# Channel attention on pairs of images, with the second image's gathers held for the next pair's first convolution

## What is computed

```python
xn = (x - mu) * rsqrt(var + EPS) * ln_g + ln_b          # mu, var over one whole image
def _proj(xn, wp, bp, wd, bd):
    y = einsum('bhcij,hoc->bhoij', xh, wp) + bp         # 8 heads of 12 channels
    return dwconv3x3(y, wd, bd)
Q, K, V = _proj(xn, ..q..), _proj(xn, ..k..), _proj(xn, ..v..)
logits = einsum('bhnc,bhnd->bhcd', K, Q) / alpha        # n: the 256 pixels
attn = softmax(logits, axis=-1)
out = einsum('bhnc,bhcd->bhnd', V, attn)
return einsum('bcij,oc->boij', out, w_f) + b_f + xn
```

## Time and profile before

| | |
|---|---|
| median of 3 runs | 494.51 us |
| lowest and highest | 494.37 and 496.22 us |
| the profiled execution | 495.76 us |
| its span, first to last instruction | 494.1 us |
| granted TensorE clock, mean of the span | 0.993 |
| busy: PE, DVE, ACT, POOL | 473.8, 363.1, 303.3, 188.6 us |
| last stage | from 331.44 us on |

### The profile page before, as it was taken

The page is one execution under the profiler, slowest core; times in us unless marked ns, Lnnn a source line. Parts: engine busy times, 40 slices in busy tenths (PEclk is TensorE's granted clock), DMA queues, the critical chain, the costliest instruction groups (busy, mean ns, idle before and its releaser), DMA issues. The chain is left out here.

```text
span 494.1 us, 27247 instructions
## 1 busy us (share of the span) xinstructions
PE 473.8 (96%) x10948; PEld 294.4 (60%) x10948; DVE 363.1 (73%) x1001; ACT 303.3 (61%) x763; POOL 188.6 (38%) x245
## 2 busy tenths in 40 slices
PE   7999999999999999999899999999999999999996
PEld 6766666666666666666665344335565555656563
DVE  1589999999999999999743476647765656566544
ACT  2477888878888888887545747634444444444332
POOL 8534344343444444444344204522332323232300
PEclk8899999999999999999999999999999999999999
DMA  4211112111111101100013223875544344444411
GB/s 79 68 40 25 27 34 51 32 23 26 33 32 32 24 24 32 46 2 4 4 44 92 50 70 78 181 142 114 127 115 125 103 122 107 118 108 117 119 31 35
DMA packets 40987, 32.54 MB, mean 66 GB/s; under 512 B 19240, under 2 KB 36776, under 8 KB 40936
## 3 DMA queue, kind: packets, MB, share of 16 engines
q1 hardware_dynamic: 36968, 25.32, 20.6%
q0 software_dynamic: 3968, 6.51, 6.1%
HBM read 18.36 MB, written 7.13 MB: 52 GB/s over the span
## 5 line engine op out<-in xcount | busy, mean ns | idle before, releaser
L414 POOL TENSOR_TENSOR scores<-scores,peak 128x768 f32<-128x768 f32 x64 | 94.3, 1474 | 124.6 <-DVE peak L583 124.6
L1644 PE MATMUL ps_hidden<-x_stack,conv_w 40*32 40x256 f32 x3072 | 97.4, 379 | 0.3 <-issue 0.3
L1050 POOL DMA_DIRECT2D x_stack<-padded_x x96 | 52.4, 548 | 102.8 <-PE ps_hidden L1644 74.5
L1644 PEld LDWEIGHTS ps_hidden<-x_stack,conv_w 40*32 40x32 f32 x3072 | 52.6, 105 | 27.4 <-issue 12.1
L477 ACT COPY probs_t<-ps_probs 128x768 f32<-128x768 f32 x64 | 51.1, 799 | 28.9 <-PE ps_probs L738 28.9
L575 DVE TENSOR_TENSOR scores<-ps_scores,bias 128x768 f32<-128x768 f32 x64 | 61.2, 957 | 3.6 <-PE ps_scores L728 3.2
L583 DVE TENSOR_REDUCE peak<-scores 128x12 f32<-128x768 f32 x64 | 61.0, 953 | 2.4
L471 ACT ACTIVATE scores<-scores 128x768 f32<-128x768 f32 x64 | 54.3, 848 | 1.6 <-POOL scores L414 1.6
L738 PE MATMUL ps_probs<-ident,scores 128*128 128x128 f32 x384 | 54.0, 277 | 0.1
L728 PE MATMUL ps_scores<-k_blocks,q_sb 32*64 32x256 f32 x768 | 43.4, 398 | 6.4 <-issue 6.3
L738 PEld LDWEIGHTS ps_probs<-ident,scores 128*128 128x128 f32 x384 | 41.6, 141 | 2.1 <-issue 0.8
(11 more groups left out here) (164 smaller groups left out, 825.2 us busy)
## 6 DMA issues: line engine op xcount, KB each, us to landing
x_stack<-padded_x POOLq DMA_DIRECT2D x96, 54.0 KB, 2.8
x_stack<-padded_x SPq DMA_DIRECT2D x96, 54.0 KB
padded_x<-x_pad SPq DMA_DIRECT2D x32, 121.5 KB, 2.5
stream<-y_sliced SPq DMA_DIRECT2D x48, 64.0 KB, 2.6
out<-y_sb SPq DMA_DIRECT2D x32, 96.0 KB, 2.0
x_now<-in_x SPq DMA_DIRECT2D x32, 72.0 KB, 1.8
stream<-in_x SPq DMA_DIRECT2D x32, 72.0 KB, 1.9
x_sliced<-stream SPq DMA_DIRECT2D x36, 64.0 KB, 2.0
```

Source lines behind the costliest of these rows:

```text
L414: nc.gpsimd.tensor_tensor(sc, sc, peak[:, par, p, :].unsqueeze(2).to_broadcast((128, HEADS, WN)), ALU.subtract).then_inc(s["shifted"], 1)
L1050: engine.dma_start(last.x_stack[64 * half + i * HC:64 * half + (i + 1) * HC, slot, :, :], rows).then_inc(landed[slot], 16)
L1644: mm = nc.tensor.matmul(ps[32 * k:32 * k + 32, r, :], conv_w[rows, kind, j, k, :], grid(x_stack[rows, slot, k, :], PADW)[:, :, j:j + W], s ...
```

## The change

The stage now takes pairs of images: 16 steps n in place of 32, images 2n and 2n+1 in each. Each operation of the stage is as before but for both images: the copies take 1024 columns (L1543, L1548, L1610) or 512 (L1557), the softmax four head groups, `finalise` one matmul of 512 columns (L1715), `finish` 512 columns into `y_sb` (L1638), and the store both images (L1498, 192 KB). The convolution of a pair is 48 matmuls of 256 columns (L1670), the transposes are 8 (L1688), `attend` 4 matmuls (L1709), gram 32 (L1699). To make room, q and k, v, the tokens and the attended product live in half of the MLP's `hidden` buffer; the gram matrix moves to the `ps_y` banks.

`finalise` stands before the second convolution, where it stood behind it. On VectorE, `finish` of the pair before stands between the subtraction of the peak and the softmax's sum. On SP, the gather of image 0 of pair n+2 waits for `v_ready` of pair n as before; then comes the store of pair n-1; then the gather of image 1 of pair n+2, which waits for the first convolution of pair n+1 (`qk_ready`); then both padded writes of pair n+3. On GpSimd the two gathers follow each other with the same waits, and no store. TensorE waits for both images' gathers in `await_taps`. The core of the diff:

```diff
+def pair_loop(engine, step):
+    for n in range(2):
+        step(n, 0, n)
+    with engine.Fori(1, STEPS // 2 - 2) as i:
+        for par in range(2):
+            step(i * 2 + par, i, par)
+    for n in range(STEPS - 4, STEPS):
+        step(n, n // 2, n % 2)
...
 def gather_taps(engine, last, t, lap, slot, half, landed):
-    need(engine, last.v_ready, t - SLOTS + 1)
     engine.wait_ge(last.written[slot], (lap + 1) * 16)
...
-        def step(t, lap, slot):
-            if not past(t + SLOTS):
-                gather_taps(sp, last, t + SLOTS, lap + 1, slot, 0, stacked_sp)
-            if not is_image(t, 0):
-                store(t - 1, 1 - slot % 2)
-            if not past(t + AHEAD):
-                write_padded(sp, last, t + AHEAD, (slot + AHEAD) % SLOTS)
+        def step(n, lap, par):
+            if not over(n + 2):
+                need(sp, s["v_ready"], n + 1)
+                gather_pair(sp, place(n, 0, lap, par, SLOTS), 0, stacked_sp)
+            if not is_image(n, 0):
+                store(n - 1, 1 - par)
+            if not over(n + 2):
+                sp.wait_ge(s["qk_ready"], n + 2)
+                gather_pair(sp, place(n, 1, lap, par, SLOTS), 0, stacked_sp)
+            if not over(n + 3):
+                for e in range(PAIR):
+                    t, _, slot = place(n, e, lap, par, AHEAD)
+                    write_padded(sp, last, t, slot)
...
     def run_pool(pool):
+        def step(n, lap, par):
+            if not over(n + 2):
+                need(pool, s["v_ready"], n + 1)
+                gather_pair(pool, place(n, 0, lap, par, SLOTS), 1, stacked_pool)
+                pool.wait_ge(s["qk_ready"], n + 2)
+                gather_pair(pool, place(n, 1, lap, par, SLOTS), 1, stacked_pool)
...
+        def step(n, lap, par):
+            copy_v(n, par)
+            if not is_image(n, 0):
+                copy_av(n - 1)
+            if not over(n + 3):
+                for e in range(PAIR):
+                    t, later, slot = place(n, e, lap, par, AHEAD)
+                    pad_image(nc, act, last, stream, t, later, slot)
+            if not over(n + 1):
+                copy_qk(n + 1)
+            exponent(n)
...
+        def step(n, lap, par):
+            copy_tokens(n)
+            if not over(n + 3):
+                normalise_pair(n + 3, 1 - par)
+            shift_logits(n)
...
+            if not is_image(n, 0):
+                finish(n - 1, lap if par else lap - 1, 1 - par)
+            normalise(n)
...
+        def await_taps(n, lap, par):
+
+            for e in range(PAIR):
+                pe.wait_ge(stacked_sp[PAIR * par + e], (lap + 1) * 16 * SIDE)
+                pe.wait_ge(stacked_pool[PAIR * par + e], (lap + 1) * 16 * SIDE)
+            need(pe, s["qk_copied"], n)
...
+        def step(n, lap, par):
+            turn_tokens(n)
+            if not over(n + 1):
+                await_taps(n + 1, lap + par, 1 - par)
...
+            if not is_image(n, 0):
+                attend(n - 1, 1 - par)
+            if not over(n + 1):
+                convolve(1 - par, 0, ps_qk, s["qk_ready"])
...
+            gram(n)
+            if not over(n + 1):
+                pe.wait_ge(s["v_copied"], n + 1)
+            if not is_image(n, 0):
+                finalise(n - 1)
+            if not over(n + 1):
+                convolve(1 - par, 1, ps_v, s["v_ready"])
```

More of the change, by code:

```diff
@@ L1428, with over, channel_attention @@
 ZEROED = 4 + TILE_HEADS
[L1431 to L1442, removed]
+PAIR = 2
+STEPS = B // PAIR
+def pair_loop(engine, step):
[6 more added lines that the diff above has]
+        step(n, n // 2, n % 2)
+def over(n):
+    return isinstance(n, int) and n >= STEPS
+def channel_attention(nc, ctx, sem, stream, stats, ident, average, w, eps, s2, last, banks, spare, out):
     def sb(name, shape, dt=F32):
@@ L1495, in run_sp, with gather_pair @@
+        pair_loop(sp, step)
+        store(STEPS - 1, 1)
         for par in range(2):
-            sp.wait_ge(out_done[par], 16 * (B // 2))
+            sp.wait_ge(out_done[par], 16 * (STEPS // 2))
+    def gather_pair(engine, where, half, landed):
+        t, lap, slot = where
+        gather_taps(engine, last, t, lap, slot, half, landed)
     def run_pool(pool):
-        def step(t, lap, slot):
-            if not past(t + SLOTS):
-                gather_taps(pool, last, t + SLOTS, lap + 1, slot, 1, stacked_pool)
@@ L1555, in step @@
                 act.wait_ge(last.moments_set, 24)
-        lap_loop(act, step)
-        copy_av(B - 1)
+            if not over(n + 4):
+                take_moment(n + 4, par)
+        pair_loop(act, step)
+        copy_av(STEPS - 1)
     def run_dve(dve):
@@ L1663, in gram @@
-        def gram(t):
-            pe.wait_ge(s["tok_copied"], t + 1)
-            need(pe, s["shifted"], t)
-            for r in range(ROUNDS):
-                for n in range(2):
-                    for k in range(TILE_HEADS):
-                        mm = nc.tensor.matmul(ps_gram[32 * k:32 * k + 32, r, :], tokens[:, n, r, 32 * k:32 * k + 32],
-                                              tokens[:, n, r, 32 * k + HC:32 * k + 2 * HC], start=(n == 0), stop=(n == 1))
-            mm.then_inc(s["gram_ready"], 1)
@@ new lines, in gram @@
+        def gram(n):
+            pe.wait_ge(s["tok_copied"], n + 1)
+            need(pe, s["shifted"], n)
+            for e in range(PAIR):
+                for r in range(ROUNDS):
+                    for h in range(2):
+                        for k in range(TILE_HEADS):
+                            mm = nc.tensor.matmul(ps_gram[32 * k:32 * k + 32, ROUNDS * e + r, :], tokens[:, e, h, r, 32 * k:32 * k + 32],
+                                                  tokens[:, e, h, r, 32 * k + HC:32 * k + 2 * HC], start=(h == 0), stop=(h == 1))
+            mm.then_inc(s["gram_ready"], 1)
```

298 lines of the change are left out of this document (132 added, 166 removed).

## The result

The changed kernel takes 516.99 us (median of 4 runs, 513.44 to 520.01), the kernel before 494.44 beside it. The ratio is 1.043, with a 95% interval of 1.039 to 1.047. Forecast were 508.7 us and a range of 502 to 515, so the direction was right and the size too small by 8.3 us. The profiled execution is the longest of the four, 520.01 us, with a span of 518.3.

A forecast was written before the change was run, and what follows sets the result against it. TensorE alone was taken to bound the last stage before the change, a late gather behind the store after it. 357.53 + 12 x 10.83 = 487.5, + 9.16 = 496.65, + 11.6 = span 508.25; forecast 508.7 us, range 502 to 515.

The forecast's parts named there:

- the chain: Last stage: final matmul, y_sb, SP's store, second gather, next attend; 6.34 us against TensorE's 4.67, a period of 10.83.
- a landing: From the third issue of SP's gather to its landing: taken as 2.4 us, in the middle of 2.0 and 2.8.
- the rival that names the other side: Faster: the gathers are there in time and TensorE's 9.16 us a pair stands, 486.9 us; chance 6%.
- TensorE's own pair: TensorE's work for one pair of images in the last stage, without waits: 9.16 us, against 9.81 before.
- the serial end of 11.6: End of the last stage: the last pair's copies, softmax, attend, final matmul, y_sb and store in series, 11.6 us.
- a stall of 1.67 us: TensorE's idle time before the attend matmuls: 6.34 us of waiting path against 4.67 of work, in 13 steps.
- a granted clock below 1.00 in the stage: Listed as a sign that would prove the forecast wrong: TensorE's clock under its upper level in the last stage.
- start of the stage to the first attend: From 331.44 to the first attend at 346.1, waiting for image 5's gather, landed at 346.0.
- first to second attend: One period of 10.83 us plus 0.6 for the moments of the last 16 images: second attend at 357.53.
- 12 periods: Steps after the second attend that await gathers: 12 periods of 10.83 us, from 357.53 to 487.5.
- last pair's period: The last pair's attend place has no gather to wait for: 9.16 us, to 496.65.

The follow-up runs named there:

- e1: The changed kernel with SP issuing both images' gathers of a step ahead of the store, all waits kept: 490.27 us, ratio 0.990.
- e2: The changed kernel without the two waits on the first convolution (SP and GpSimd), gather still behind the store: 515.09 us, ratio 1.041.
- e4: The changed kernel with SP's two padded writes ahead of the second gather: 564.95 us, ratio 1.142.
- e6: e4 plus 14 unused matmuls of 96 columns before the wait for the gathers, in the loop's steps only: 538.92 us, ratio 1.088.
- e3: The changed kernel with nine unused matmuls of 96 columns ahead of each attend from step 1 on: 516.53 us, ratio 1.048.
- e5: The changed kernel with eight unused matmuls of 96 columns before the wait for the gathers, in the loop's steps only: 515.21 us, ratio 1.034.
- e10: e1 with the wait on the next pair's first convolution kept on both queues in step 0 alone: 493.00 us, ratio 0.995.

## Why the prediction was right, and where it was wrong

**Right: what bounds, and the chain.** The gather behind the store is what TensorE waits for, 1.4 to 1.7 us in most steps of the loop, GpSimd's is not late, and a period takes 10.84 to 10.98 us for 10.83. The single links are off by 0.01 to 0.10: 1.34 for 1.29, 0.90 for 0.91, 0.67 for 0.60, 0.98 for 1.01, and landing with semaphore 2.63 for 2.53. The choice of 2.4 for a landing that the trace didn't show was good (2.5 by the row at 431.55). The estimate of 2.1 us that the prediction weighed, from the Trainium skill ("DMA: Bandwidth & Descriptors", "Anatomy of one DMA"), would have been short by 0.4. The section gives its numbers for DMAs issued from GpSimd, and the gather of the chain is SyncE's; GpSimd's own land in 2.6 us in this trace. e1 and e2 show that the chain is the cause: the order alone takes the stall away, the wait alone doesn't.

**Right: the rival that names the other side.** TensorE's own pair was put at 9.16 and is 9.23 (e1). Terms of that sum are off both ways: 1.03 for the transposes and for the final matmul (0.97 and 0.94), 0.66 for gram (0.72). That rival's time of 486.9 us is 3.4 below e1's 490.27. In e1's profile the first attend is 1.0 us later than the rival has it, the periods hold 1.5 us more, and the end 1.6 more, with the clock low from 482.5 on.

**Wrong: the clock.** The step that failed is that every term of the stage, the periods of 10.83 us and the serial end of 11.6, was priced at the upper clock, as if a stall of 1.67 us cost only itself. The prediction named "a granted clock below 1.00 in the stage" as something that would prove it wrong and gave it neither a price nor a chance. It is the larger part of what is missing: 7.1 us in two periods and 1.6 at the end, of 10.1. Against the forecast span of 508.25, the trace of the changed kernel has 518.3:

| term | forecast | measured | difference |
|---|---|---|---|
| start of the stage to the first attend (from 331.44; 331.42) | 346.1 | 347.30 | +1.2 |
| first to second attend | 11.43 | 11.24 | -0.2 |
| 12 periods | 129.96 | 136.52 | +6.6 |
| last pair's period | 9.16 | 10.22 | +1.1 |
| end | 11.6 | 13.0 | +1.4 |

Two of the twelve periods, 14.84 and 14.02, hold 7.1 us more than 10.9 each; the written-out 10.03 and 10.10 take 1.5 us back. The clock does the 7.1: the stretch from 370 us has a clock of 0.54 and the convolution is 5.37 long. That such falls come of the stall is shown by e4 and e6, on the longer stall: with 2.9 us the clock is down for half of the time, and filling it with useless matmuls is worth 26 us. For the changed kernel's own stall, e3 and e5 have the upper clock through the whole loop, in one profile each, but their totals don't settle how many us that is worth. Which executions meet a fall, and when, differs: the changed kernel's four runs spread over 6.6 us (513.44 to 520.01), with mean clocks from 0.988 down to 0.970 in that order, where the four of the kernel before keep within 2.0. TensorE's page of the Trainium skill ("TensorE: Matmul & The Clock Gate", section "A second HAM failure mode: psum-queue depth-cycling") tells of a kernel in which short idle times between groups of matmuls, if frequent, let the clock swing between its levels. This trace agrees, with stalls of 1.5 to 2.1 us; the page gives no price for them, and I had not weighed it.

**Mis-sized: the start.** The first attend waited for no gather at all: it came when TensorE reached it. The convolutions of the ramp are longer than 2.76, because TensorE stands still in their middle:

```profile
331.42 4.91 PE L1670 MATMUL ps_hidden<-x_stack,conv_w 40*32 40x256 f32 x163 [0.31 <-issue]
336.60 1.09 PE L1670 MATMUL ps_hidden<-x_stack,conv_w 40*32 40x256 f32 x29 [0.28 <-issue]
...
342.62 1.93 PE L1670 MATMUL ps_hidden<-x_stack,conv_w 40*32 40x256 f32 x57
344.85 1.50 PE L1670 MATMUL ps_hidden<-x_stack,conv_w 40*32 40x256 f32 x39 [0.30 <-issue]
```

TensorE reached the place 2.2 us later than the 345.1 that was worked out, later than the 346.1 worked out for the gather. Such gaps come at the same records in e1 and e10 (57 and 39), just behind a transfer of 16 KB on the queue for instructions.

Nor did the gather set the second attend. It was released by ScalarE's copy of q and k, which stood behind the moments:

```profile
358.54 1.08 PE L1709 MATMUL ps_y<-hidden,attn 128*64 128x256 f32 x8 [1.38 <-ACT hidden L1548]
```

By the 2.63 us of the loop the gather was due at 358.4 (an estimate), so this other path cost next to nothing, and 11.24 for 11.43 came out near by another wait than the one forecast.

**Mis-sized: the last period and the end.** The last pair's convolutions take 3.37 and 3.12 us from start to start, not 2.75 (rows at 496.08 and 501.14 below). They have gaps like those of the start, at the upper clock, and not in every profile: the same period is 10.22 us here, but 9.22 in e2, which has the same order, and 9.23 in e1. And the end runs at the lower clock:

```profile
496.08 3.44 PE L1670 MATMUL ps_hidden<-x_stack,conv_w 40*32 40x256 f32 x96
...
501.14 3.19 PE L1670 MATMUL ps_hidden<-x_stack,conv_w 40*32 40x256 f32 x96
...
510.43 1.80 PE L1709 MATMUL ps_y<-hidden,attn 128*64 128x256 f32 x8 [2.00 <-DVE attn L1629]
512.92 2.02 PE L1715 MATMUL ps_y<-hidden,final_w 128*96 128x512 f32 x2 [0.68 <-ACT hidden L1557]
```

Attend takes 1.80 and the final matmul 2.02 us where 1.08 and 1.10 are theirs at the upper clock: +1.6, a little more than the whole difference of the end. The serial waits up to the last attend took 5.15 us for 5.7 worked out, and the time behind the last y_sb 2.6 for 2.2; the two nearly cancel.

**The range.** Its upper end, 515, was made of a longer landing (2.8), and the landing wasn't longer. Had the clock been a term, with one or two falls of the size measured (3.1 and 3.9 us), the forecast would have been 512 to 516, still a little under the 516.99; the start and the last period are the rest.

## What to carry to other kernels

A DMA that the bounding engine waits for stands ahead of any DMA on the same in-order queue that waits for a result of the same step; here that order decides between 1% faster and 4% slower. Where a forecast has a short, regular stall of TensorE, its price is not the stall alone: read the granted clock, and give a fall of the clock a term and a chance. When an operation is moved ahead to release a waiting engine, look at everything that engine waits for, shared PSUM banks too.

## What the runs showed of the hardware that I had not expected

- TensorE's clock fell from 2.4 to 1.2 GHz in kernels whose only idle times were short ones: with stalls of 1.4 to 2.1 us in periods of 10.9 it fell twice in the changed kernel's twelve periods and once in e2's, with stalls of 2.9 us in 12.2 it was down for half of the time, and with periods of 9.23 and no stall it never fell in the loop (seven profiles). A low stretch lasted 3.4 to 20.5 us in these stages.
- Matmuls that compute nothing made a kernel faster: by 26 us in e6 against e4. For e5 against the changed kernel it is not settled: 1.034 against 1.043 without e5's two longest executions, 1.8 us by the medians of all.
- The links of the chain are shorter outside the hardware loop. In the written-out step at 484.96 the final matmul is 1.14 us ahead of y_sb (1.34 in the loop), y_sb 0.77 ahead of the store (0.90), and the store 0.44 ahead of the gather (0.67), so the period is 10.10. Why was not tried.
- TensorE can stand inside a group of equal matmuls that wait for nothing, 0.3 to 1.7 us, just behind a transfer of 16 KB on the queue for instructions. That it waits for instructions there is a reading, not tested. The gap in the third convolution was longer with more gathers under way: 0.31 to 0.86 in the five kernels that issue the gathers first and keep the wait in step 0, 1.67 and 1.68 in the two without it. That the gathers lengthen it was not tested by itself.
